# Last layer, second matmul: the inverse weight scales go into weights split in two parts, the activations are split as whole numbers, and ScalarE and GpSimd finish the sums

## What is computed

```python
def quantize_w8_per(w, axis):
    amax = jnp.clip(jnp.max(jnp.abs(w), axis=axis, keepdims=True), 1e-08, None)
    scale = 127.0 / amax
    w_q = jnp.clip(jnp.round(w * scale), -128.0, 127.0) / scale
    return _ste(w, w_q)
def quantize_a16(x):
    amax = jnp.clip(jnp.max(jnp.abs(x)), 1e-08, None)
    scale = 32767.0 / amax
    x_q = jnp.clip(jnp.round(x * scale), -32768.0, 32767.0) / scale
    return _ste(x, x_q)
W_in_sim = quantize_w8_per(W_in, axis=0)
W_out_sim = quantize_w8_per(W_out, axis=1)      # one scale for each of the 1024 hidden features
hidden = jax.nn.gelu(quantize_a16(x) @ W_in_sim + b_in, approximate=False)
out = quantize_a16(hidden) @ W_out_sim + b_out  # and then x + out
```

## Time and profile before

| | |
|---|---|
| median of 3 runs | 3632.83 us (3630.29 to 3636.98) |
| the profiled execution's own time | 3637.8 us |
| its span, first to last instruction | 3635.9 us |
| mean granted TensorE clock | 0.968 of full speed |
| busy share of PE, DVE, ACT, POOL over the span | 92%, 66%, 46%, 33% |
| the last block | from about 3516.3 us to the end, some 119.6 us |

### The profile page before, as it was taken

One profiled execution on the slowest core, in us unless ns is written; L12 is line 12 of the kernel. 1 busy time (PEld: TensorE's weight loads), 2 busy tenths in 40 slices (PEclk: granted clock), 3 DMA queues, 4 the chain that ended last, 5 costly groups with the idle time before them and its releaser, 6 DMA issues. The chain is left out here.

```text
span 3635.9 us, 49119 instructions
## 1 busy us (share of the span) xinstructions
PE 3342.1 (92%) x14300; PEld 1881.8 (52%) x14300; DVE 2393.1 (66%) x3634; ACT 1674.5 (46%) x1904; POOL 1207.1 (33%) x545
## 2 busy tenths in 40 slices
PE   6999999999999999999999868799999999999576
PEld 4445445455454464454464445455555555554366
DVE  4665665665656656656646524687788778777699
ACT  3442442443433433434434312366566566566376
POOL 2563663554645545636546613100000000000101
PEclk9999999999999999999999989799999999999698
DMA  7444544444534435535445232344344343343202
GB/s 183 122 119 117 121 121 103 121 109 126 121 101 123 120 101 133 122 99 125 108 118 128 68 110 79 75 105 106 72 102 104 79 103 96 89 101 82 65 18 75
DMA packets 265102, 379.08 MB, mean 104 GB/s; under 512 B 35944, under 2 KB 170672, under 8 KB 265008
## 3 DMA queue, kind: packets, MB, share of 16 engines
q1 hardware_dynamic: 265008, 378.06, 41.2%
HBM read 82.22 MB, written 27.26 MB: 30 GB/s over the span
## 5 line engine op out<-in xcount | busy, mean ns | idle before, releaser
L839 POOL TENSOR_TENSOR a_prob_sum<-a_prob_sum,a_prob 128x1024 f32<-128x1024 f32 x384 | 915.8, 2385 | 420.4 <-ACT a_prob L576 409.6
L576 ACT ACTIVATE a_prob<-a_t 128x1024 f32<-128x1024 f32 x512 | 518.8, 1025 | 752.9 <-PE a_t L430 739.5
L1590 DVE TENSOR_REDUCE a_mhalves<-a_m 128x1 f32<-128x512 f32 x1024 | 689.9, 688 | 188.2 <-PE a_m L1341 185.2
L718 DVE TENSOR_REDUCE a_mhalves<-a_m 128x1 f32<-128x512 f32 x1024 | 671.0, 688 | 165.0 <-PE a_m L397 161.8
L1502 ACT ACTIVATE a_prob<-a_t 128x1024 f32<-128x1024 f32 x512 | 498.3, 1023 | 145.5 <-PE a_t L1361 140.2
L397 PE MATMUL a_m<-a_kh_n,a_qz 128*128 128x512 f32 x1024 | 445.1, 457 | 64.1 <-DVE a_kl_n L707 29.3
L1341 PE MATMUL a_m<-a_vh,a_qz 128*128 128x512 f32 x1024 | 463.5, 464 | 36.6 <-DVE a_mhalves L1590 19.7
L437 PE MATMUL a_o<-a_prob,a_v_pair 128*64 128x512 f32 x2048 | 495.7, 605 | 0.0
L732 DVE RECIPROCAL a_recip<-a_x 128x512 f32<-128x512 f32 x64 | 214.8, 3357 | 349.0 <-PE a_x L446 349.0
L397 PEld LDWEIGHTS a_m<-a_kh_n,a_qz 128*128 128x128 f32 x1024 | 186.3, 192 | 367.9 <-DVE a_mhalves L718 223.5
L422 PE MATMUL a_t<-a_q_hl,a_k_hh 128*128 128x512 f32 x1024 | 360.3, 433 | 8.0 <-DVE a_x_res L787 8.0
(11 more groups left out here) (242 smaller groups left out, 4081.2 us busy)
## 6 DMA issues: line engine op xcount, KB each, us to landing
a_k_hh<-a_kh_n SPq DMA_DIRECT2D x256, 256.0 KB, 4.5
a_k_lm<-a_kl_n SPq DMA_DIRECT2D x128, 256.0 KB, 4.2
a_v_pair<-a_v_all SPq DMA_DIRECT2D x64, 512.0 KB, 3.9
a_vs<-a_vh SPq DMA_DIRECT2D x256, 128.0 KB, 2.3
a_wk<-wk_parts SPq DMA_DIRECT2D x64, 256.0 KB, 3.5
a_q_hl<-a_qz SPq DMA_DIRECT2D x128, 128.0 KB, 3.3
a_q_hm<-a_qz SPq DMA_DIRECT2D x128, 128.0 KB, 3.7
a_q_hl<-a_ql_n SPq DMA_DIRECT2D x128, 128.0 KB, 4.2
```

Source lines behind the costliest of these rows:

```text
L576: nc.scalar.activation(prob[:, t % RING], ps_t[t % 2][:, :, :], ACT.Exp, scale=SCALE0).then_inc(s_exp, 1)
L718: nc.vector.tensor_reduce(mhalves[:, qt, hd, n:n + 1], ps_m[:, n, :], AX.X, ALU.max).then_inc(s_max, 1)
L839: nc.gpsimd.tensor_tensor(acc, prob[:, (t - 1) % RING] if t == 1 else acc, prob[:, t % RING], ALU.add).then_inc(s_acc, 1)
L1590: nc.vector.tensor_reduce(mhalfs[:, u, qt, h, k:k + 1], ps_m[:, k, :], AX.X, ALU.max).then_inc(s_max, 1)
```

## The change

`wout_inv` leaves the activations and goes into the weights. At the block's start VectorE multiplies the whole weights by it, tile by tile, into `wo_whole` (which is `spare`), ScalarE rounds that to `wo_high`, and VectorE makes the remainder `wo_low`. The activations are now split as whole numbers, straight from `hid`: `h_int` is gone, `h_high` is one ScalarE instruction a chunk and `h_low` one VectorE instruction a chunk. The scaling of a chunk moves from VectorE to a ScalarE instruction in place (`scaled`), and VectorE keeps two instructions for clip and round that follow right behind each other; it works two chunks ahead instead of three. TensorE does three matmuls for each group of queries and tile instead of two (high with high, high with low weights, low with high): 24 a chunk, 96 a batch. It waits for a chunk where it waited for a tile. ScalarE takes the sums of a batch out of PSUM, times the inverse scale, into `y_sb` (`keep_y`), and GpSimd adds that to `xo` (`finish`, one instruction a batch). The last two batches are stored whole.

The core of the diff:

```diff
-        AHEAD = 3
-        h_int = sb("h_int", [P, FFT, NQ])
+        AHEAD = 2
+        wo_high = sb("wo_high", [P, FFT, D], F32R)
+        wo_low = sb("wo_low", [P, FFT, D], F32R)
+        wo_whole = spare
+        y_sb = sb("y_sb", [P, QT, D])
...
                 for b in (B - 2, B - 1):
-                    for qt in range(0, QT, 2):
-                        sp.wait_ge(s_o, QT * b + qt + 2)
-                        sp.dma_start(out_view[:, b * QT + qt:b * QT + qt + 2, :], xo[:, b % 2, qt:qt + 2]
-                                     ).then_inc(s_st[b % 2], 16)
+                    sp.wait_ge(s_o, b + 1)
+                    sp.dma_start(out_view[:, b * QT:(b + 1) * QT, :], xo[:, b % 2]).then_inc(s_st[b % 2], 16)
...
             def _(dve):
+                def rounded(b, k):
+                    cols = tiles(b, CT * k, CT)
+                    dve.wait_ge(s_sc, CH * b + k + 1)
+                    nc.vector.tensor_scalar(cols, cols, 32767.0, -32768.0, ALU.min, ALU.max).then_inc(s_r, 1)
+                    dve.wait_ge(s_r, 2 * (CH * b + k) + 1)
+                    nc.vector.tensor_scalar(cols, cols, MAGIC, None, ALU.add).then_inc(s_r, 1)
+                def low(b, k):
+                    dve.wait_ge(s_high, CH * b + k + 1)
+                    nc.vector.scalar_tensor_tensor(chunk(h_low, k), tiles(b, CT * k, CT), MAGIC, chunk(h_high, k),
+                                                   ALU.subtract, ALU.subtract).then_inc(s_low, 1)
+                def batch(b, after):
+                    for k in range(CH):
+                        low(b, k)
+                        if k < CH - AHEAD:
+                            rounded(b, k + AHEAD)
+                        elif after:
+                            rounded(b + 1, k + AHEAD - CH)
+                rounded(0, 0)
+                for ft in range(FFT):
+                    nc.vector.tensor_scalar(wo_whole[:, ft, :], wout[:, ft, :].bitcast(F32), wout_inv[:, ft:ft + 1],
+                                            None, ALU.mult).then_inc(s_ww, 1)
+                rounded(0, 1)
+                dve.wait_ge(s_wh, 1)
+                nc.vector.tensor_tensor(wo_low[:], wo_whole[:], wo_high[:], ALU.subtract).then_inc(s_wl, 1)
...
             def _(act):
+                def scaled(b, k):
+                    cols = tiles(b, CT * k, CT)
+                    nc.scalar.activation(cols, cols, ACT.Copy, scale=amax["h"][4][:]).then_inc(s_sc, 1)
+                def high(b, k):
+                    if not (isinstance(b, int) and b == 0):
+                        if k < CH - 1:
+                            act.wait_ge(s_used, (CH - 1) * (b - 1) + k + 1)
+                        else:
+                            act.wait_ge(s_y, b)
+                    act.wait_ge(s_r, 2 * (CH * b + k + 1))
+                    whole = hid[:, CT * k:CT * (k + 1), bass.ds((b + 1) * NQ - NQ, NQ)]
+                    nc.scalar.activation(chunk(h_high, k), whole, ACT.Identity,
+                                         bias=minus_magic[:]).then_inc(s_high, 1)
+                def keep_y(b, u):
+                    act.wait_ge(s_y, b + 1)
+                    if not (isinstance(b, int) and b == 0):
+                        act.wait_ge(s_o, b)
+                    nc.scalar.activation(y_sb[:], ps_y[:, u, :, 0:D], ACT.Copy, scale=amax["h"][5][:]
+                                         ).then_inc(s_ys, 1)
                 def batch(b, u, before, after):
                     for k in range(CH):
+                        if k < CH - AHEAD - 1:
+                            scaled(b, k + AHEAD + 1)
+                        elif after:
+                            scaled(b + 1, k + AHEAD + 1 - CH)
+                        high(b, k)
+                        if before and k == 1:
+                            keep_y(b - 1, 1 - u)
+                for k in range(AHEAD + 1):
+                    scaled(0, k)
+                    if k == 1:
+                        act.wait_ge(s_ww, FFT)
+                        nc.scalar.copy(wo_high[:], wo_whole[:]).then_inc(s_wh, 1)
...
             def _(pool):
+                def finish(b, u):
+                    pool.wait_ge(s_ys, b + 1)
+                    pool.wait_ge(s_b, b + 1)
+                    nc.gpsimd.tensor_tensor(xo[:, u], xo[:, u], y_sb[:], ALU.add).then_inc(s_o, 1)
...
             def _(pe):
-                        pe.wait_ge(s_o, QT * (b - 1))
+                        pe.wait_ge(s_ys, b - 1)
...
-                            pe.matmul(sums, h_high[:, ft, queries], weights,
-                                      start=(ft == 0), stop=False)
-                            mm = pe.matmul(sums, h_low[:, ft, queries], weights,
+                            pe.matmul(sums, h_high[:, ft, queries], wo_high[:, ft, :], start=(ft == 0), stop=False)
+                            pe.matmul(sums, h_high[:, ft, queries], wo_low[:, ft, :], start=False, stop=False)
+                            mm = pe.matmul(sums, h_low[:, ft, queries], wo_high[:, ft, :],
                                            start=False, stop=(ft == FFT - 1))
...
+                pe.wait_ge(s_wl, 1)
```

More of the change, by code:

```diff
@@ L2051, in quantised_layer @@
         s_y = sem("y_projected")
+        s_ys = sem("y_scaled")
         s_o = sem("out_ready")
@@ L2056, in tiles, with chunk @@
             return hid[:, first:first + n, bass.ds(b * NQ, NQ)]
+        def chunk(t, k):
+            return t[:, CT * k:CT * (k + 1), :]
         with nc.Block() as block:
@@ new lines, in _ @@
+                rounded(0, 0)
[5 more added lines that the diff above has]
+                nc.vector.tensor_tensor(wo_low[:], wo_whole[:], wo_high[:], ALU.subtract).then_inc(s_wl, 1)
+                batch(0, True)
+                with dve.Fori(1, B - 1) as b:
+                    batch(b, True)
@@ L2129, in _ @@
+                batch(B - 1, False)
             @block.scalar
             def _(act):
[L2131 to L2138, removed]
+                def scaled(b, k):
+                    cols = tiles(b, CT * k, CT)
+                    nc.scalar.activation(cols, cols, ACT.Copy, scale=amax["h"][4][:]).then_inc(s_sc, 1)
@@ L2153, in batch @@
+                def batch(b, u, before, after):
                     for k in range(CH):
-                        if k < CH - 1:
-                            whole(b, k + 1)
+                        if k < CH - AHEAD - 1:
+                            scaled(b, k + AHEAD + 1)
                         elif after:
-                            whole(b + 1, 0)
+                            scaled(b + 1, k + AHEAD + 1 - CH)
                         high(b, k)
-                whole(0, 0)
-                batch(0, True)
@@ L2162, in _ @@
-                with act.Fori(1, B - 1) as b:
-                    batch(b, True)
-                batch(B - 1, False)
+                        if before and k == 1:
[5 more added lines that the diff above has]
+                        nc.scalar.copy(wo_high[:], wo_whole[:]).then_inc(s_wh, 1)
+                batch(0, 0, False, True)
@@ L2166, in _ @@
+                with act.Fori(0, B // 2 - 1) as i:
+                    batch(2 * i + 1, 1, True, True)
+                    batch(2 * i + 2, 0, True, True)
+                batch(B - 1, 1, True, False)
+                keep_y(B - 1, 1)
             @block.gpsimd
             def _(pool):
-                with pool.Fori(0, B // 2) as i:
+                def finish(b, u):
+                    pool.wait_ge(s_ys, b + 1)
+                    pool.wait_ge(s_b, b + 1)
+                    nc.gpsimd.tensor_tensor(xo[:, u], xo[:, u], y_sb[:], ALU.add).then_inc(s_o, 1)
@@ L2169, in _, with add_bias @@
+                def add_bias(u, count):
+                    pool.wait_ge(s_xl[u], 16 * count)
+                    nc.gpsimd.tensor_tensor(xo[:, u], xo[:, u], bout[:].unsqueeze(1).to_broadcast([P, QT, D]),
+                                            ALU.add).then_inc(s_b, 1)
+                add_bias(0, 1)
+                add_bias(1, 1)
+                with pool.Fori(0, B // 2 - 1) as i:
                     for u in range(2):
-                        pool.wait_ge(s_xl[u], 16 * (i + 1))
-                        nc.gpsimd.tensor_tensor(xo[:, u], xo[:, u], bout[:].unsqueeze(1).to_broadcast([P, QT, D]),
-                                                ALU.add).then_inc(s_b, 1)
+                        finish(2 * i + u, u)
+                        add_bias(u, i + 2)
@@ L2174, in _ @@
+                finish(B - 2, 0)
+                finish(B - 1, 1)
             @block.tensor
```

40 lines of the change are left out of this document (11 added, 29 removed).

## The result

| | before | changed |
|---|---|---|
| median (6 runs each) | 3632.83 us | 3652.34 us (3648.30 to 3654.82) |
| profiled execution: own time, span | 3637.8, 3635.9 us | 3654.5, 3652.7 us |
| granted TensorE clock, mean | 0.968 | 0.968 |

The ratio is 1.0051, 95% interval 1.0039 to 1.0064: slower, by 14 to 23 us. The forecast was 3644.5 in a range of 3634 to 3657.

A forecast was written before the change was run, and what follows sets the result against it. VectorE was taken to set the last block's pace, by its own work plus waits for GpSimd's adds. Start +5.1, middle +2.4 and end +4.2 sum to +11.7 us on the 3632.8 median: 3644.5, range 3634 to 3657.

The forecast's parts named there:

- VectorE's own work falls to 9.92 a batch: VectorE, last block: a chunk takes 2.48 us and `finish` goes, so its work falls from 11.93 to 9.92 us.
- Each finishing add holds VectorE for 2.12: GpSimd's new add, once a batch, makes VectorE wait 2.12 us, as the bias add does; bounds 0 and 2.9.
- The start, +5.1: Block's start: first remainder of activations ends at 3531.8 instead of 3526.71, +5.1 us; bounds 0.9 and 7.
- ScalarE and TensorE hidden, count 0: Middle batches: TensorE's 12.8 us and ScalarE's 9.5 stay under VectorE's 14.16, so their waits add 0.
- the middle term: From the first remainder's end to the last one's: 103.2 us instead of 100.8, +2.4 us.
- about 0.8 us to spare: Third chunk's remainder due after 6.8 us; TensorE needs 2.8, then ScalarE 3 x 1.05, leaving about 0.8 us.
- its sign of being wrong: Wrong if VectorE idles behind `h_high`, batches take 12 to 13 us, or the block's clock falls far under 0.85.
- The end, +4.2: From the last remainder to the block's end: 12.6 us instead of 8.35, +4.2 us.
- The term behind the last matmul: Block's end: `keep_y` 1.05, an add of 2.4, a store of 3.0 plus about 0.6, together 7.1 us.
- the 8.35 I compared with: Kernel before: 8.35 us from the last remainder to the end, taken from the profiled execution.
- Rival A: The new adds do not hold VectorE; TensorE sets the batch at 12.8 us: +2.2, 3635.0 us; chance 0.12.
- Rival C: TensorE becomes the bound at half clock, 20.4 us a batch: about 3686 us; chance 0.06.

The follow-up runs named there:

- the second profile: The changed kernel profiled once more, nothing edited: own time 3649.0 us, block 132.5 us.
- the first pair: First profiles of the kernel before and the changed kernel, nothing edited: blocks 120.0 and 134.9 us, own times 3637.8 and 3654.5 us.
- the first experiment: GpSimd's finishing add cut to one column of 1024, against the changed kernel: block 117.1 us, own time 3633.8 us.
- the first profile: The changed kernel's first profiled execution, nothing edited: own time 3654.5 us, block 134.9 us.
- the later ones: Medians of the changed kernel against the kernel before in five more rounds: 3649.4 us beside 3634.8, ratio 1.0038.

## Why the prediction was right, and where it was off

The direction, its cause and the range hold. By its own steps:

- *VectorE's own work falls to 9.92 a batch*: right, 2.47 a chunk. The dependent pair costs 0.72 + 0.61 (3569.21 to 3569.93 to 3570.54), as read from the earlier trace rows; what the Trainium skill says under "The DRAIN you can't avoid" in VectorE: DVE Perf Modes, that the semaphore costs nothing, would have made the chunk 0.12 shorter, and the trace does not agree.
- *Each finishing add holds VectorE for 2.12*: right. 2.1 to 2.2 in the rows, about as much each when taken away and when doubled, and the holds of the bias adds are the same. SBUF — State Buffer of the Trainium skill ("Who interferes with whom") names the lock; its whole length is not quite what VectorE loses: in the rows above the clip ends 0.54 us behind the add (3574.58, 3574.04) where it needs 0.69, as if its first 0.15 us had gone on beside the add (GpSimd's ends are rough in a profile, so this is not shown).
- *The start, +5.1*: +4.7, with the two bias adds on its path.
- *ScalarE and TensorE hidden, count 0*: this step failed, in the middle term: +4.1 to +5.2 instead of +2.4. I set "about 0.8 us to spare" between `keep_y` and the next remainder, with TensorE at full clock and on time. In the first batch it is neither: it begins at the half clock and with each chunk ready faster (2.47) than it can take it (2.9 at full clock). From the end of that batch's last remainder (3540.62) TensorE needed 7.2 us to the sums (3547.83), where 2.8 were counted, and ScalarE 3.2 behind it. VectorE came for the third remainder after 6.3 us (3546.88), not 6.8: three chunks of 2.48 less the 1.15 of the last remainder give 6.3 already, so even by the forecast's own figures 0.3 us was to spare. 7.2 + 3.2 - 6.3 gives 4.1, the wait of 4.18 up to rounding. So ScalarE's `keep_y` passes TensorE's lateness on to VectorE, 3.3 to 4.2 us. The prediction had named this path, and counted it in the upper end of its range; its sign of being wrong, VectorE idle behind `h_high`, showed in this one place. In the later batches the holds give TensorE time, and VectorE never waits: the step is right there. One finishing add falls into that wait and so costs nothing, which takes 1.9 back.
- *The end, +4.2*: +5.0 and +6.2. The term behind the last matmul was right (7.1 expected, 6.9 from the start of `keep_y` at 3645.73). At full clock TensorE took 5.1 us behind the last remainder (the second profile), and in the first 6.4 in place of 5.5: it had idled 2.8 us behind the last two holds, and began its last three chunks (3635.52) at the half clock. What made the clock fall there stays open: the second profile has the same idle time of 2.8 us ahead of its last three chunks (3631.30), and went through them at full clock. And the 8.35 I compared with was itself an end at half clock; with full clock on both sides it is 5.8 against 12.1, and the difference 6.2. So I set a mean clock for the one against the slow clock of the other. That the first pair came near the forecast is luck: both of its ends were slow.
- *Rival A*, no hold, has its condition refuted for six adds of seven. Its case was made in the first experiment: there TensorE was busy for 73 of 75 us (3545 to 3620), and the middle took 91.3. *Rival C* is refuted: the clock is 1.00 from 3545 to 3635 in the first profile, and in the second VectorE has no wait behind either of two half-clock stretches of 3.4 us (from 3575.3 and 3602.6).

The profiled blocks differ by 15 us, the first medians by 19.5 and the later ones by 14.6; both intervals hold 15. The point forecast, 3644.5, lies 7.8 us under the first median and 4.9 under the later one. By the blocks the size missed is 3.2 or 3.4 us of 15. In the first pair of profiles 2.8 of it lies in the middle and 0.8 at the end; in the second, with full clock at both ends, 1.7 in the middle and 2.0 at the end. The start gives 0.4 back in both. Nothing in the runs points to a cause ahead of the block.

## What to carry to other kernels

Look at what shares a resource with the engine that sets the pace before handing its work to an idle one: here 1.57 us of VectorE's own work became 2.15 us of VectorE waiting. An instruction that lasts four times its twins, with no wait shown, points to such a resource; look at what ran on the other engines at that moment, and move that, before thinning the long one. And where an engine in order copies results for another, check its place against the consumer's worst moment, the first batch at half clock, not against the steady state.

## What the runs showed that I had not expected

The end of the same kernel can differ by 2.6 us between two executions by the granted clock alone (0.50 or 1.00 for nearly all of the last 32 matmuls, with the same idle times ahead of them to 0.1 us), while its start and middle agree to 0.01 us. And a GpSimd add of 128x1024 that falls into VectorE's idle time costs 0.24 us, not 2.15: the price hangs on the moment, so three adds in a row cost three times 2.15 only because VectorE had work each time.
